# Sixteen-step attention kernel: one row tile of x split earlier, one rounded later, the second query's lows moved behind four maxima, and halves of output tiles moved in the last steps

## The reference

```python
def cond(x, a):        # per batch a LoRA adapter of rank 16
    return x @ W.T + b + (x @ lora_As[a]) @ lora_Bs[a] * 2
def attn(x):           # 32 query heads and 8 key/value heads of 32
    q, k, v = x @ w_q, x @ w_k, x @ w_v
    return softmax(q @ k.T / sqrt(32)) @ v @ w_o
x = x + attn(cond(x, itok_B_0_23))
h = einsum('bsi,boi->bso', x, weight[itok_B_3_7])     # one 1024 x 1024 matrix per batch
gates = softmax(keep_top_2(h @ router_w.T))           # 4 experts
x = x + einsum('te,ter,eor->to', gates, h @ A, B) * 4 # rank-16 experts
```

## Time and profile before

| | |
|---|---|
| median of 3 runs | 1009.52 us |
| the profiled execution | 1010.05 us, its span 1008.4 us |
| PE busy | 987.5 us (98%), granted clock 0.998 of full speed |
| DVE, ACT, POOL busy | 62%, 45%, 25% |
| chain that ended last | PE 92%, DVE 4%, ACT 1%, POOL 1%, issue 1%, DMA 1% |
| step 0 of attention begins | 187.6 us |
| steps 11 and 12 of pair 0 | about 262 to 276 us; pairs 1 and 2 are 129.6 us apart |
| last steps of attention and the start of the finish | about 691 to 728 us |

### The profile page before, as it was taken

One profiled execution on the slowest core, in us unless ns is written; L12 is line 12 of the kernel. 1 busy time (PEld: TensorE's weight loads), 2 busy tenths in 40 slices (PEclk: granted clock), 3 DMA queues, 4 the chain that ended last, 5 costly groups with the idle time before them and its releaser, 6 DMA issues.

```text
span 1008.4 us, 16074 instructions
## 1 busy us (share of the span) xinstructions
PE 987.5 (98%) x6228; PEld 769.9 (76%) x6228; DVE 625.9 (62%) x1028; ACT 453.6 (45%) x806; POOL 247.2 (25%) x234
## 2 busy tenths in 40 slices
PE   9999999999999999999999999999999999999996
PEld 6878788777687776877777777786787778778775
DVE  6671822686946778467786688766664654654443
ACT  6121322365744657456665566747441432332221
POOL 1000001033422434223343247645110110110001
PEclk9999999999999999999999999999999999999999
DMA  7030411111411124111142424264999579463432
GB/s 274 0 105 1 136 48 56 43 44 39 128 36 44 50 59 123 44 44 49 44 114 79 110 74 138 86 170 185 276 298 251 165 248 243 143 223 108 164 125 84
DMA packets 72395, 117.33 MB, mean 116 GB/s; under 512 B 7698, under 2 KB 55186, under 8 KB 70816
## 3 DMA queue, kind: packets, MB, share of 16 engines
q1 hardware_dynamic: 62592, 81.70, 28.5%
q0 software_dynamic: 9728, 34.61, 10.0%
HBM read 86.38 MB, written 18.89 MB: 104 GB/s over the span
## 4 chain that ended last, share of the span: by engine, by line
PE 92%; DVE 4%; ACT 1%; POOL 1%; issue 1%; DMA 1%; POOLq 0%; ACTq 0%
PE psP L854 21%; PE psW L1239 17%; PE psF L292 12%; PE psG L1284 8%; PE psO L950 6%; PE psS L926 6%; PE psT L937 5%; PE psX L1580 3%; PE psO L954 3%; DVE nmax L770 2%; PE psF L303 2%; PE psP L876 2%; DVE q_stack L739 1%; PE psP L878 1%; PE psM L961 1%; PE psP L880 1%
## 5 line engine op out<-in xcount | busy, mean ns | idle before, releaser
L630 POOL TENSOR_TENSOR p_sum<-probs 128x512 f32<-128x512 f32 x128 | 168.5, 1317 | 331.7 <-ACT probs L681 331.7
L854 PE MATMUL psP<-x_hl,wq 128*128 128x512 f32 x960 | 237.2, 391 | 0.2 <-DVE v_sb L760 0.2
L770 DVE TENSOR_REDUCE nmax<-psS 128x2 f32<-128x512 f32 x256 | 164.5, 684 | 96.2 <-PE psS L926 91.8
L854 PEld LDWEIGHTS psP<-x_hl,wq 128*128 128x128 f32 x960 | 173.4, 188 | 31.2 <-DVE v_sb L760 0.4
L681 ACT ACTIVATE probs<-psT 128x512 f32<-128x512 f32 x256 | 139.0, 595 | 74.2 <-PE psT L937 73.4
L1239 PE MATMUL psW<-o_split,wq 128*128 128x512 f32 (+1 forms) x600 | 137.5, 383 | 0.0
L1239 PEld LDWEIGHTS psW<-o_split,wq 128*128 128x128 f32 x600 | 108.8, 188 | 21.4
L1269 DVE TENSOR_TENSOR cond_lo<-cond_raw,cond_hi 128x1024 fp32r<-128x1024 f32 x64 | 78.3, 1240 | 54.8 <-ACT cond_hi L1265 54.3
L1265 ACT ACTIVATE cond_hi<-cond_raw 128x1024 fp32r<-128x1024 f32 x64 | 66.5, 1057 | 82.9 <-PE psG L1284 70.2
L739 DVE TENSOR_TENSOR q_stack<-psP,q_stack 32x512 fp32r<-32x512 f32 x128 | 87.8, 686 | 10.2 <-ACT q_stack L646 8.3
L926 PEld LDWEIGHTS psS<-k_stack,q_stack 96*128 96x128 f32 x512 | 79.0, 189 | 16.5 <-DVE q_stack L739 2.1
(11 more groups left out here) (155 smaller groups left out, 1378.4 us busy)
## 6 DMA issues: line engine op xcount, KB each, us to landing
cond_raw<-in_cond POOLq DMA_DIRECT2D x64, 512.0 KB, 4.8
x_raw<-in_xT SPq DMA_DIRECT2D x32, 256.0 KB, 3.2
o_scratch<-o_sb SPq DMA_DIRECT2D x64, 128.0 KB
q_stack<-q_stack SPq DMA_DIRECT2D x31, 256.0 KB, 2.9
q_raw<-in_Wqkv SPq DMA_DIRECT2D x24, 256.0 KB, 3.9
o_pair<-rden_scratch SPq DMA_DIRECT2D x24, 256.0 KB, 9.0
o_pair<-o_scratch SPq DMA_DIRECT2D x6, 1024.0 KB, 13.9
w_raw<-in_W SPq DMA_DIRECT2D x8, 512.0 KB, 7.8
```

Of the source, the lines that this page charges most:

```text
L630: pool.tensor_tensor(p_sum[:, heads], probs[:, 0, heads], probs[:, 1, heads], ALU.add).then_inc(sum_done, 1)
L770: dve.tensor_reduce(nmax[:, n % 2, 2 * hp:2 * hp + 2, qt], psS[:, i % 2].rearrange("p (h k) -> p h k", h=2), AX.X, ALU.max, negate=True).t ...
L854: mm = pe.matmul(out, wq[:, i, w, k * P:(k + 1) * P], x[:, k, part], start=(k == 0 and n_ == 0), stop=False)
```

## The change

Nothing is added to or taken from the computation. Four things move.

1. In `X_HI` row 4 of the next pair's x is rounded in the second half of ACT's step 11, behind the copies of q7, instead of the first half. In `X_LO` the low of row 3 is made in the first half of DVE's step 11, right behind rows 0 and 1, instead of in the second half. This is at three places (pairs 0 to 2).
2. In step 0 of attention DVE makes the lows of q1 behind the four maxima and their split; before they stood between the second and the third.
3. The halves of output tiles in the last steps: the first half of tile 7 of batch 0 goes from step 17 to step 16 (ahead of row 0), the second half from behind row 5 to step 17; the tiles of batch 1 follow half a tile earlier each. DVE's residuals move with them, and ACT copies the turned g ahead of rounding row 9.
4. POOL issues the load of row 6 ahead of its last `p_sum` (`ahead_gpsimd_last`), instead of behind it together with row 7.

```diff
-X_HI = {(10, 1): range(4), (11, 0): [4], (12, 0): [5, 6], (12, 1): [7]}
-X_LO = {(11, 0): [0, 1], (11, 1): [3], (12, 1): [5, 6], (13, 0): [7]}
+X_HI = {(10, 1): range(4), (11, 1): [4], (12, 0): [5, 6], (12, 1): [7]}
+X_LO = {(11, 0): [0, 1, 3], (12, 1): [5, 6], (13, 0): [7]}
...
                 pool.wait_ge(exp_done, TILES * n + 2 * hp + 2)
                 if n and hp == 0:
                     pool.wait_ge(pv_done, n)
+                if n == N - 1 and hp == 1:
+                    ahead.gpsimd_last(pool)
...
-            for unit_ in late(n - 1) if n else [(0, "q1")]:
+            for unit_ in late(n - 1):
                 evacuate(*unit_)
...
                 split_maxima(n)
+            if n == 0:
+                evacuate(0, "q1")
...
-            load_cond(pool, n, range(6, KT) if n == 0 else range(KT))
+            load_cond(pool, n, range(7, KT) if n == 0 else range(KT))
...
+        if part == 1 and s == 17:
+            residual(dve, KT - 1)
...
+    def ahead_gpsimd_last(pool):
+        load_cond(pool, 0, [6])
+
     def ahead_tensor(pe, n, part):
...
-        if (n - LAST, part) == (17, 0):
-            one_tile(pe, 0, KT - 1, range(4))
+        if (n - LAST, part) in ((16, 0), (17, 0)):
+            one_tile(pe, 0, KT - 1, range(4) if n - LAST == 16 else range(4, KT))
...
             cond_row_hi(act, KT)
+            turn_copies(0)
             cond_row_hi(act, KT + 1)
-            turn_copies(0)
...
             dve.memset(beats[:], 0.0).then_inc(chain, 1)
+            residual(dve, KT)
             cond_row_lo(dve, 7)
-            residual(dve, KT - 1)
...
         def second():
-            residual(dve, KT)
+            residual(dve, KT + 1)
             gates(0)
             for m in range(KT):
-                if m:
+                if m > 1:
                     residual(dve, KT + m)
...
             cond_row(pe, 5)
-            one_tile(pe, 0, KT - 1, range(4, KT))
+            one_tile(pe, 1, 0, range(4, KT))
             cond_row(pe, 6)
             cond_row(pe, 7)
-            one_tile(pe, 1, 0, range(4, KT))
+            one_tile(pe, 1, 1, range(4))
             turn_g(0)
-            one_tile(pe, 1, 1, range(4))
+            one_tile(pe, 1, 1, range(4, KT))
             middle(0)
...
             for m in range(1, KT - 1):
-                one_tile(pe, 1, m, range(4, KT) if m == 1 else range(KT))
+                if m > 1:
+                    one_tile(pe, 1, m)
                 cond_row(pe, KT + m)
```

More of the change, by code:

```diff
@@ L1683, in finish_stage @@
     ahead.sync, ahead.gpsimd, ahead.scalar, ahead.vector = ahead_sync, ahead_gpsimd, ahead_scalar, ahead_vector
-    ahead.tensor = ahead_tensor
+    ahead.tensor, ahead.gpsimd_last = ahead_tensor, ahead_gpsimd_last
     st.sync, st.gpsimd, st.scalar, st.vector, st.tensor = sync, gpsimd, scalar, vector, tensor
```

## The result

| | before | changed |
|---|---|---|
| median of 20 runs each, in turn on one chip | 1009.51 us | 1012.26 us |
| lowest, highest | 1008.21, 1012.41 | 1009.28, 1017.97 |
| ratio of the times | | 1.0031, 95% 1.0019 to 1.0044 |
| profiled execution, span | 1010.05, 1008.4 | 1009.42, 1007.7 |

The changed kernel is 0.3% slower; the forecast was 2.5 us faster, 1007.0, with a range to 1009.3. So it shows what was predicted, and only part of what went wrong; a long one comes with the last experiments.

A forecast was written before the change was run, and what follows sets the result against it. PE, occupied 987.5 of 1008.4 us, bounds the kernel, so only its waits count. Part 1 -1.8, part 2 -0.3, parts 3 and 4 -2.8 + 2.0 + 0.4: total -2.5, median 1007.0 us, range 1004.9 to 1009.3.

The forecast's parts named there:

- the stall: Ahead of PE's sums of step 15: row 6's load delays POOL's last p_sum, PE idles 2.0 us; bounds 0.5 to 2.6.
- Rival (a): At POOL's last p_sum: address work hidden in the wait, stall 0.5 instead of 2.0, total 1005.5 us; chance 0.17.
- seven places: At the end of attention: PE was said to wait at seven places of some tenths of a us.
- Nothing is priced on it: Whole kernel: the granted clock was 0.998 throughout, so no term was charged for it.
- the sum: Whole kernel: part 1 -1.8, part 2 -0.3, parts 3 and 4 together -0.4, total -2.5 us.
- Rival (c): End of attention: late step 15 sums delay the reciprocal at 718.65, then row 8's low; result 1009.6 or 1010.6; chance 0.07.
- what rows 6 and 7 return: PE's waits at rows 6 (0.89) and 7 (0.72): row 6's load no longer late, 0.4 still lost at row 7.

The follow-up runs named there:

- experiment 6: DVE's second normalisation moved one row and one residual later: in the changed kernel without part 4, 1005.79 us, ratio 0.9964; in the changed kernel 1011.25 us, 1.0013.
- experiment 1: The changed kernel with part 4 undone (row 6's load behind the last p_sum again), parts 1 to 3 kept: 1008.37 us, ratio 0.9989.
- experiment 8: Changed kernel rerun unaltered: 1015.20 us, ratio 1.0058; also half a tile put between rows 8 and 9, without part 4, normalisation later: 1005.50 us, 0.9963.
- experiment 5: SP issues batch 3's loads ahead of the reciprocals' store, or the next pair's x loads later: in the changed kernel ratios 1.0033 and 1.0005.

## Why the prediction was wrong

**Parts 1 and 2** are right: 0.6 in each pair and 0.26 by the trace, and 1.7 us faster (0.7 to 2.6) by their own kernel, against 2.1.

**Part 4, the stall.** Right in mechanism and size: 1.88 against 2.0, with the chain of register load, address work and DMA instruction as drawn. Rival (a), the cheap load, is out. (The "seven places" at which PE waits are five in the earlier trace rows; the sum names and uses five.)

**The clock.** "Nothing is priced on it" is the first failed sentence: a term put at nothing. Of the idles on PE between 700 and 755 us in these profiles, three of twelve of 1.6 to 2.0 us had half clock with or behind them, and all seven of 2.5 us and more. The changed kernel's short profiled run pays 1.4 us at the stall, its long one 2.3 at 748 us.

**The sum is the step that failed.** I added up PE's waits until 728 us and took it that what is saved there arrives at the end. It was a term left out, the load of batch 3, whose cover ran out. PE's tile at 745.58 in before needed batch 3 on DVE by about 742.9 (the tile, less 2.29 and 0.41 for the normalisation and the residual). With parts 1 to 3 that moved to 738.5 (the tile of 742.80 less its idle, less the same), with part 4's stall and no drop to 740.4 (748.47 - 5.38 - 2.70). The transfer landed at 741.0 in before, and at 740.1 and 745.7 in those two profiles: 1.9 us of slack became 1.6 and 5.3 us too late. In the kernel without part 4 the cause is tested, by the normalisation moved (experiment 6). In the changed kernel it is read from one long execution and its total; there the same move did not bring the time down, since the landing came later still and then held the low of a row. Rival (c), at 0.07, had the direction right and a chain that is late, with the wrong victim: it followed the late sums to the reciprocal at 718.65 and to the low of row 8, not to batch 3, whose loads SP issues behind the store of the reciprocals. It priced only the delay of part 4, where the earlier PE of parts 1 to 3 counts as well.

**Part 3** was priced at -2.8 before rows 6 and 7 are given back. In its profiles the waits go, and nothing arrives: 0.9989 with it, 0.9983 without it. With the normalisation moved some of it does: 0.9964 against 0.9983 for parts 1 and 2 alone, 1.9 us (between nothing and 5, if the bounds of the two are set against each other), though that edit was not tried on parts 1 and 2 alone. That "only between rows 8 and 9 none are left" puts two 512 KB loads close together, but giving the half tile back changed neither the landing (740.1 as in experiment 1) nor the ratio (0.9963).

**Part 4's price** was +2.0 less what rows 6 and 7 return. It is 4.2 by the ratios with and without it (1.0031, 0.9989; between 1.3 and 7.1 by their bounds), and 8 us alone.

**Open.** Why the transfers land up to 9 us later with part 4 in is not settled. The traces narrow it. In the long execution of experiment 8, against that of experiment 1, the last denominators are stored 1.9 us later (707.74, 705.80), their load lands 5.0 later (718.6, 713.6), the store of the reciprocals is issued 5.0 later, the last load of batch 3 is issued 3.5 later (724.92, 721.46) and takes 20.8 us instead of 18.6. But the store in front is not all of it: with the loads of batch 3 ahead of it (experiment 5) the changed kernel stays at 1.0033. The other thing is how far ahead of POOL's load of row 12 that last load of batch 3 goes out. Where row 12 follows 6.7 us behind, it takes 11.6 us to land; at 2.3 to 3.6 us behind, 16.7 to 17.3 (three profiles); at 1.1 to 1.5, 18.2 to 19.6 (nine profiles, and 16.4 in that of parts 1 and 2 alone); at 0.53 or less, or with row 12 first, 20.6 to 22.4 (six). An earlier PE brings row 12's load forward and a late sum holds batch 3's back, so both halves of the change push the same way. That is a pattern over twenty profiles; no run here sets this distance by itself. The clock's own price in the medians isn't settled either.

## What to carry to other kernels

An engine that becomes earlier runs into transfers that don't: for each load behind the change, compute the time by which its consumer needs it, not only the waits that the profile shows. A wait of zero has a slack that the DMA view gives: here the load landed at 741.0 and PE's tile needed it by 742.9, 1.9 us, and parts 1 to 3 moved that need 4.4 us forward and the landing 0.9. Put an instruction that waits for a long transfer behind the ones that free the busy engine's buffers, on every in-order queue. And compare executions of the same length: a long one of one kernel beside a short one of another shows a difference that is not the edit's.

## What the hardware showed that I had not expected

An idle of 1.9 us on PE draws half clock in some executions and none in others of the same program: the changed kernel's two profiles have the same stall, 1.88 and 1.89, one with 0.50 behind it and one with 1.00. In the kernel with part 4 alone half clock lasted ten microseconds with PE busy in all of them behind the idle, through 32 products of 68 columns, a row and half a tile. And the execution with half clock at the stall was the short one. That it made PE 1.8 us later is not what spared it: its transfer landed at 740.4, and PE's tile, at 744.91, needed it by 742.2, so 1.8 us earlier it would have been just in time. What differed is the landing, 5.3 us later in the long one.
